# Cross-attention kernel: where the softmax's row sums are summed over partitions

## The reference

```python
memory_proj = jnp.einsum('bme,de->bmd', memory, W_mem)
scores = jnp.einsum('bnd,bmd->bnm', hidden_states, memory_proj) / jnp.sqrt(jnp.float32(D))
attn = jax.nn.softmax(scores, axis=-1)
memory_context = jnp.einsum('bnm,bmd->bnd', attn, memory_proj)
gate_input = jnp.concatenate([hidden_states, memory_context], axis=-1)
gate = jax.nn.sigmoid(jnp.einsum('bnf,df->bnd', gate_input, W_gate) + b_gate)
fused = hidden_states + gate * memory_context
return _rmsnorm(fused, norm_w)
```

## Time and profile before

| | us |
|---|---|
| median of 3 runs | 537.66 |
| lowest and highest | 537.37 and 537.76 |
| profiled execution, its own time | 537.72 |
| its span (first to last instruction) | 535.9 |
| mean granted TensorE clock | 0.996 of full speed |

### The profile page before, as it was taken

How to read it: one execution, slowest core, us unless ns; L and a number is a source line. 1 busy time by engine, 2 the same in 40 slices (tenths; PEclk the granted TensorE clock), 3 DMA queues, 4 the chain that set the end, 5 groups by cost and what they waited for, 6 DMA issues and landing times.

```text
span 535.9 us, 8824 instructions
## 1 busy us (share of the span) xinstructions
PE 524.8 (98%) x2364; PEld 431.7 (81%) x2364; DVE 482.8 (90%) x797; ACT 323.2 (60%) x614; POOL 172.2 (32%) x129
## 2 busy tenths in 40 slices
PE   8998999999999999999999999999999999999994
PEld 7876888888888888888888888888888888888883
DVE  3799958999799998999989998899979999899967
ACT  4675636676467655686465863666557765558524
POOL 0004610185004740066200950027400573008702
PEclk9999999999999999999999999999999999999998
DMA  9967263511687027840378105870267502401033
GB/s 226 269 122 125 64 102 91 100 40 31 181 164 130 20 59 168 177 81 20 112 149 185 39 20 173 148 144 21 75 153 167 110 20 76 141 31 39 2 117 119
DMA packets 186118, 56.38 MB, mean 105 GB/s; under 512 B 161756, under 2 KB 175592, under 8 KB 186100
## 3 DMA queue, kind: packets, MB, share of 16 engines
q1 hardware_dynamic: 185572, 55.64, 44.7%
q10 hardware_dynamic: 528, 0.52, 0.3%
HBM read 46.15 MB, written 8.39 MB: 102 GB/s over the span
## 4 chain that ended last, share of the span: by engine, by line
PE 93%; DVE 4%; DMA 1%; issue 1%; ACT 1%; SPq 0%; POOLq 0%; POOL 0%; DVEq 0%
PE bank L391 22%; PE bank L393 21%; PE bank L392 21%; PE bank L567 8%; PE bank L568 8%; PE bank L569 8%; PE bank L470 1%; DMA mem_raw<-in_ctx_dram 1%; PE bank L551 1%; PE bank L550 1%; PE bank L603 0%; DVE wg1t_lo L904 0%; DVE p_lo L904 0%; DVE fused L1081 0%; SPq L339 0%
## 5 line engine op out<-in xcount | busy, mean ns | idle before, releaser
L1256 POOL TENSOR_TENSOR psum_rows<-psum_rows,p_tmp 128x512 f32<-128x512 f32 (+1 forms) x88 | 129.6, 1473 | 39.5 <-ACT p_tmp L735 36.1
L904 DVE TENSOR_TENSOR p_lo<-p_tmp,p_hi 128x512 fp32r<-128x512 f32 (+1 forms) x104 | 89.2, 858 | 5.9 <-ACT p_hi L696 5.9
L1267 POOL TENSOR_TENSOR fused<-fused,x_again 128x512 f32<-128x512 f32 x14 | 17.9, 1300 | 219.1 <-DVE fused L1077 219.1
L391 PE MATMUL bank<-q_hi,mt_hi 128*128 128x512 f32 (+1 forms) x208 | 81.9, 394 | 0.0
L393 PE MATMUL bank<-q_hi,mt_lo 128*128 128x512 f32 (+1 forms) x208 | 81.3, 391 | 0.0
L392 PE MATMUL bank<-q_lo,mt_hi 128*128 128x512 f32 (+1 forms) x208 | 81.2, 390 | 0.0
L735 ACT ACTIVATE p_tmp<-s 128x512 f32<-128x512 f32 (+1 forms) x104 | 64.4, 626 | 27.6 <-DVE s L968 26.5
L567 PE MATMUL bank<-p_hi,mem_hi 128*128 128x512 f32 (+1 forms) x196 | 76.4, 390 | 0.0
L568 PE MATMUL bank<-p_lo,mem_hi 128*128 128x512 f32 (+1 forms) x196 | 76.3, 390 | 0.0
L569 PE MATMUL bank<-p_hi,mem_lo 128*128 128x512 f32 (+1 forms) x196 | 76.3, 389 | 0.0
L696 ACT ACTIVATE s<-bank 128x512 f32<-128x512 f32 (+1 forms) x104 | 62.0, 596 | 19.1 <-PE bank L393 18.7
(11 more groups left out here) (105 smaller groups left out, 1024.7 us busy)
## 6 DMA issues: line engine op xcount, KB each, us to landing
mem_raw<-in_ctx_dram SPq DMA_DIRECT2D x48, 256.0 KB, 3.0
mem_blocks<-in_ctx_dram SPq DMA_DIRECT2D x64, 136.0 KB
x_again<-in_x_dram SPq DMA_DIRECT2D x32, 256.0 KB, 2.8
out_dram<-fused SPq DMA_DIRECT2D x32, 256.0 KB, 2.1
x_raw<-in_x_dram SPq DMA_DIRECT2D x112, 64.0 KB, 2.0
mem_blocks<-in_ctx_dram SPq DMA_DIRECT2D x56, 64.0 KB, 2.0
x_raw<-in_x_dram SPq DMA_DIRECT2D x4, 256.0 KB, 4.9
gate<-in_L_xattn_W_gate_dram SPq DMA_DIRECT2D x2, 512.0 KB, 5.9
```

What stands on the lines that cost most here:

```text
L391: nc.tensor.matmul(dst, a_hi, b_hi, start=(start and i == 0), stop=False)
L904: return nc.vector.tensor_tensor(dst, src, hi.bitcast(F32), ALU.subtract)
L1256: nc.gpsimd.tensor_tensor(psum_rows[0:r, :], a, p_tmp[0:r, t % TMP_RING, :], ALU.add).then_inc(p_added, 1)
```

## The change

The 128 partial sums of a query row are added by VectorE instead of TensorE for batches 0 to 6. `transpose_sums(b)` transposes `psum_rows` in 32 x 32 blocks into PSUM bank 7, between the low parts of q and of U at the end of pass b. In pass b + 1, among the scores, `reduce_sums` (pair 1) sums each block's rows to a 128 x 16 tile, `join_sums` (pair 3) adds the upper and lower half of the partitions to 64 x 16 and then, in four additions of 32 x 4, the two quarters, each written to another quarter of `p_total` (128 x 4), and `reciprocal` (pair 5) reads that from SBUF. `row_sums` behind the scores is gone on TensorE, and `reciprocal` is gone from behind `column_max`. The last batch keeps its row sums on TensorE. A context product 1 now waits for the reduce (both use bank 7), and GpSimd's first addition of a batch waits for the transpose.

```diff
@@ buffers, bank, semaphores @@
+        sum_parts = sb("sum_parts", [P, N // BLOCK])
+        sum_pairs = sb("sum_pairs", [P // 2, N // BLOCK])
+        p_total = sb("p_total", [P, NT])
+        SUM_BANK = 7
+        sum_blocks, sum_reduced, sum_paired, summed = (
+            sem("sum_blocks"), sem("sum_reduced"), sem("sum_paired"), sem("summed"))
@@ TensorE @@
-            def row_sums(b, behind_scores):
+            def row_sums(b):
                 pe.wait_ge(p_added, (MT - 1) * (b + 1))
-                if behind_scores:
-                    pe.wait_ge(s_copied, MT * (b + 1) + MT - 2)
-                else:
-                    pe.wait_ge(shifted, MT * (b + 1))
+                pe.wait_ge(shifted, MT * (b + 1))
...
             def context(b, j, tail=False, halves=range(CT)):
+                if j == 1 and not tail:
+                    pe.wait_ge(sum_reduced, b + 1)
...
                 else:
-                    row_sums(b - 1, True)
                     gate_context(b - 1, 0)
@@ VectorE @@
-            def reciprocal(b):
-                dve.wait_ge(pe_sum, b + 1)
-                nc.vector.reciprocal(r_sum[:, :], bank[MAX_BANK][:, 0:NT]).then_inc(r_first, 1)
+            def transpose_sums(b):
+                dve.wait_ge(p_added, (MT - 1) * (b + 1))
+                dve.wait_ge(xt_has_lo, DT * (b + 2))
+                nc.vector.transpose(blocks(bank[SUM_BANK][:, :]), blocks(psum_rows[:, :])).then_inc(sum_blocks, 1)
+
+            def reduce_sums(b):
+                dve.wait_ge(sum_blocks, b + 1)
+                nc.vector.tensor_reduce(sum_parts[:, :], blocks(bank[SUM_BANK][:, :]), AX.X, ALU.add).then_inc(sum_reduced, 1)
+
+            def join_sums(b):
+                dve.wait_ge(sum_reduced, b + 1)
+                nc.vector.tensor_tensor(sum_pairs[:, :], sum_parts[0 : P // 2, :], sum_parts[P // 2 : P, :],
+                                        ALU.add).then_inc(sum_paired, 1)
+                dve.wait_ge(sum_paired, b + 1)
+                pairs = sum_pairs[:, :].rearrange("p (j a) -> p a j", a=BLOCKS)
+                for a in range(BLOCKS):
+                    nc.vector.tensor_tensor(p_total[a * BLOCK : (a + 1) * BLOCK, :], pairs[0:BLOCK, a, :],
+                                            pairs[BLOCK : 2 * BLOCK, a, :], ALU.add).then_inc(summed, 1)
+
+            def reciprocal(b, tail=False):
+                if tail:
+                    dve.wait_ge(pe_sum, 1)
+                    total = bank[MAX_BANK][:, 0:NT]
+                else:
+                    dve.wait_ge(summed, BLOCKS * (b + 1))
+                    total = p_total[:, :]
+                nc.vector.reciprocal(r_sum[:, :], total).then_inc(r_first, 1)
...
                         running_max(b, 2 * p + 1)
+                    if not first and p == 1:
+                        reduce_sums(b - 1)
+                    if not first and p == 3:
+                        join_sums(b - 1)
+                    if not first and p == 5:
+                        reciprocal(b - 1)
...
                     column_max(b)
-                    reciprocal(b - 1)
                     gate_input(b - 1, 0)
...
+                if not last:
+                    transpose_sums(b)
                 for c in range(CT):
                     u_lo_part(b, c)
@@ GpSimd, add_p @@
-                        pool.wait_ge(pe_sum, b)
+                        pool.wait_ge(sum_blocks, b)
```

More of the change, by code:

```diff
@@ L654, in iteration @@
                         if c == 0:
-                            row_sums(b, False)
+                            row_sums(b)
             pe.wait_ge(ready_ident, 1)
@@ L904, in lo_part, with blocks @@
                 return nc.vector.tensor_tensor(dst, src, hi.bitcast(F32), ALU.subtract)
+            def blocks(ap):
+                return ap.rearrange("p (r i) -> p r i", i=BLOCK)
             def running_max(b, t):
@@ L929, in mem_lo_part @@
                 lo_part(mem_lo[0:r, ts, :], mem_raw[0:r, raw, :], mem_hi[0:r, ts, :]).then_inc(mem_has_lo, 1)
-            def blocks(ap):
-                return ap.rearrange("p (r i) -> p r i", i=BLOCK)
             def column_max(b):
@@ L1214, in _ @@
             iteration(B - 1, False, True)
-            reciprocal(B - 1)
+            reciprocal(B - 1, True)
             gate_input(B - 1, 0, True)
```

## The result

The changed kernel takes 532.83 us (median of 4 runs, 532.78 to 532.91); the kernel before, beside it, 537.71.

What follows compares the result with a forecast made beforehand. TensorE bounds the kernel until VectorE's chain is as long. Per pass -0.89 + 0.17 = -0.72, six of them -4.3, the last pass -0.13: together -4.4, from 537.72 and 537.66 to 533.3 us; range 531.5 to 536.3.

Steps and rivals of the forecast that it cites:

- TensorE's slot: Behind the scores on TensorE: removing the eight small row-sum products saves 0.89 us a pass, in 7 passes.
- Lateness at the first gate input: VectorE's chain from the score start reaches the first gate input 0.46 us later; bounds -0.1 and 0.75.
- air: Among the scores, VectorE's gaps from waiting on score copies, together 1.03 us, set against 1.83 of inserted work.
- The bound of -0.1 for overlapping joins: At the first gate input: VectorE's lateness in us if the five joins overlap, spaced 0.12 each.
- Third gate product: TensorE's load there needs gate input 0: slack 1.18, TensorE 0.89 earlier, VectorE 0.46 later, so a stall of 0.17.
- Tail: Last pass, first tail gate product waits for u_lo: lateness 0.46 less slack 0.59, so -0.13 us.
- Contention: In the softmax, VectorE's mem_lo starts 0.03 before GpSimd's addition, so p_lo ends 0.62 earlier; VectorE's chain is -0.16 late.
- GpSimd first: Rival, softmax: GpSimd's addition gets the memory before mem_lo, VectorE 1.02 late, over 0.96: 538.0, dearer form 541.7; chance 0.18.
- contention unchanged: Rival, softmax: GpSimd and VectorE collide as before, lateness 0.46 stays, -0.50 a pass: 534.6; chance 0.12.
- The joins overlap: Rival, VectorE's five joins among the scores: lateness -0.1, no stall anywhere, 531.7; chance 0.10.
- The 0.96 at the score start: Slack in us between the first q_lo's end and when TensorE's load for the next score start needs it.
- The transpose at the end of a pass: VectorE's 0.7 us between q_lo and u_lo, covered by u_lo's 1 us wait for ScalarE: no cost, else up to 0.6.

Runs made afterwards that it cites:

- the sums left out: Changed kernel without VectorE's block transpose, reduce and joins, and no row sums on TensorE in their place; output not normalised by the true sums: 531.99 us.
- the joins uncrossed: Changed kernel with five joins of the same sizes that all read and write from partition 0 on, so the sums are wrong: 531.72 us.
- the sums early: Changed kernel with reduce and joins moved directly behind the first memory transpose of a pass, where VectorE waits for ScalarE: 531.54 us.

## Why the prediction was right

- **TensorE's slot.** This held. The stream is 0.89 shorter, and two runs without any wait of TensorE in the loop (the sums left out, the joins uncrossed) have passes of 62.26 for 63.16.
- **Lateness at the first gate input.** The prediction said 0.46 and 0.31 was measured, inside its bounds. Its parts are the reduce with +0.49 (151.62 - 150.43, less 0.70) for +0.50, the joins with +0.95 for +1.00, and the reciprocal with +0.28 for +0.33, since the low part of the memory followed the half after 0.08. Against these stand air of 1.07 for 1.03, and behind the maxima 0.34 as forecast. The air is what is left of the sum, not a reading of its own. Each term had been taken to the dear side. The joins are held, as the row of the copy and the reciprocal let expect, and their crossing of partitions accounts for 0.58 of their 0.95. The bound of -0.1 for overlapping joins was too cautious: uncrossed, the lateness is -0.26.
- **Third gate product.** The wait is there. The load is 0.14 later than it could be, of which 0.11 is given back, so 0.03 is lost at once. The next seven products follow a little more than 0.226 apart, and behind them TensorE is 0.06 behind its stream in the run without VectorE's sums; the prediction had no term for this. A pass lost 0.06 to 0.07 of its 0.89, and not the 0.17 that was forecast. This term, by the lateness, makes most of the 0.5 us between 533.3 and 532.8. It is 6 x 0.11, less the 0.07 of the next point and less the 0.2 by which the first pass began later, which leaves 0.4.
- **Tail.** It brought 0.06 and not 0.13. The lateness in the last pass was 0.58 (first gate input 22.57 after the score start, before 21.99), where I had taken over the loop's 0.46. By the prediction's own sum 0.58 would leave -0.01, so 0.05 of the gain has another source, which is open. The traces of the two kernels show where the 0.27 lie that the lateness has more than in the loop. In the last pass of the changed kernel VectorE's first mt_lo comes 0.07 later than in the loop. Behind tile 10 and behind tile 12 the operation that needs the running maximum follows after 0.78, where the loop has 0.72 and 0.71. The kernel before had been 0.07 earlier there than in its loop. Why a dependent operation follows later in the last pass is open.
- **Contention.** The forecast said that VectorE is first by 0.03, and it is by 0.08, with one long p_lo fewer and mem_lo at 0.66. The smaller lateness is not the reason: the prediction let TensorE gain at most 1.18 on VectorE, and that limit holds for any lateness at which the third gate product waits. Measured against the score start, GpSimd's addition comes 0.83 earlier and mem_lo 0.30 later, 1.13 in all; the missing 0.05 is mostly what TensorE loses behind its wait. The prediction said that a margin of 0.03 is smaller than the errors of its numbers, and gave the other order 0.18; that VectorE came first is therefore in part luck. The rival "GpSimd first", made to happen by a delay of 0.3, takes 537.8, for which the prediction had said 538.0, so its mechanism and its price were right. That an operation with one SBUF input is held too was not foreseen, and no step of the sum rested on it. No run tests "contention unchanged" (534.6) by itself; the p_lo of 0.66 speaks against it.
- **The joins overlap** (531.7) was ruled out as a fact of these joins and right as a price: made to overlap, they give 531.72.
- **Slacks.** The 0.96 at the score start is borne out by the 0.45 that is left, and by the 0.15 a pass that a reduce of 0.60 costs. The transpose at the end of a pass cost nothing, as forecast: it took the place of 0.88 in which u_lo had waited for ScalarE.

## What to carry to other kernels

Work moved to an engine that is nearly as busy is free as long as its chain between two hand-overs stays under a slack. Read that slack at the load that waits, not in the busy share. Look then at what the shorter stream of one engine does to the phase of two others that hold each other up. Here 5 us hung on whether GpSimd or VectorE starts first, by 0.08 us. A version should be given a wider margin on purpose: with the sums early it is 0.56 or more in every pass of the loop. Put small operations that cross partitions where their engine waits anyway.

## What the runs showed of the hardware

- A copy on VectorE of 64 x 16 from SBUF to SBUF waits out an addition of GpSimd that is under way (1.15 and 1.29 us instead of 0.17); the same copy out of PSUM does not (0.17).
- When a VectorE operation with two SBUF inputs (128 x 512) comes second to GpSimd's addition, it ends 0.55 after it. When it comes first, by as little as 0.08, it takes its 0.66 and GpSimd's addition 1.74 instead of 1.30.
- Small operations on VectorE that cross partitions follow each other after 0.19, others that do not depend on each other after 0.08.
